# Message pass of a graph kernel: the repeat-redirected cells of a tile are written ahead of the scan, with one semaphore for each slot of their ring

## What is computed

```python
# layer 1 (message pass), batch norm over all edges inside _mlp
node_feat = _mlp(x, W_node, b_node, g_node, beta_node)
edge_feat = _mlp(edge_attr, W_edge, b_edge, g_edge, beta_edge)
message = concatenate([x[row], x[col], edge_feat], axis=1)
message = _mlp(message, W_msg, b_msg, g_msg, beta_msg)
agg = segment_sum(message, col)
# layers 2 and 3: two SAGE convolutions each, over the same edges
agg = segment_sum(x[src], dst) / max(degree, 1);  out = agg @ Wl.T + b + x @ Wr.T
```

## Time and profile before

| | us |
|---|---|
| median of 3 runs | 5384.24 (5378.25 to 5390.44) |
| the profiled execution | 5342.66 |
| its span | 5340.8 |
| its message pass, 1474 to 3361 | 1887 |
| PE / DVE / ACT / POOL busy over the span | 3187.4 / 2666.4 / 1564.4 / 2506.9 |

### The profile page before, as it was taken

One profiled execution on the slowest core, in us unless ns is written; L12 is line 12 of the kernel. 1 busy time (PEld: TensorE's weight loads), 2 busy tenths in 40 slices (PEclk: granted clock), 3 DMA queues, 4 the chain that ended last, 5 costly groups with the idle time before them and its releaser, 6 DMA issues.

```text
span 5340.8 us, 69053 instructions
## 1 busy us (share of the span) xinstructions
PE 3187.4 (60%) x18737; PEld 2331.0 (44%) x18737; DVE 2666.4 (50%) x5882; ACT 1564.4 (29%) x3677; POOL 2506.9 (47%) x2580
## 2 busy tenths in 40 slices
PE   1555555553755555455455555311129999999999
PEld 0333333332633333333333334210017777778777
DVE  4888888886554555445454554700001154433333
ACT  1777777773222222222222222200000011111000
POOL 7666666664455565556556565777750000000000
PEclk9999999999966666666766676555559999999999
DMA  5565555653233344333344334200017756676776
GB/s 186 192 199 195 197 197 192 202 195 104 57 101 104 100 107 103 102 101 100 104 105 103 101 99 109 81 2 0 12 37 266 256 197 248 234 262 250 257 274 230
DMA packets 387448, 796.21 MB, mean 149 GB/s; under 512 B 207412, under 2 KB 264600, under 8 KB 361128
## 3 DMA queue, kind: packets, MB, share of 16 engines
q1 hardware_dynamic: 239330, 586.35, 32.8%
q0 software_dynamic: 82320, 90.28, 8.3%
q10 hardware_dynamic: 65718, 118.62, 5.8%
HBM read 581.03 MB, written 213.92 MB: 149 GB/s over the span
## 4 chain that ended last, share of the span: by engine, by line
PE 29%; issue 17%; another core or an unknown queue 14%; DVE 5%; ACT 3%; SPq 3%; DMA 1%; ACTq 1%; DVEq 0%; POOL 0%
PE ps L1166 17%; PE ps L1096 6%; SPq L633 2%; ACT ps L1215 2%; PE ps L920 1%; PE ps L927 1%; PE ps L926 1%; DVE area L1664 1%; DVE second L1629 1%; ACT out_ring L1239 1%; DMA attr<-attr_parts 1%; ACTq L1241 1%; ACT dump L1219 1%; PE ps L1049 1%
## 5 line engine op out<-in xcount | busy, mean ns | idle before, releaser
L779 POOL DMA_INDIRECT area<-relu_table,early x784 | 741.5, 946 | 400.6 <-issue 214.9
L938 PE MATMUL ps<-ident,area 96*128 96x96 f32 x2352 | 436.4, 353 | 801.5 <-issue 296.0
L779 POOL DMA_INDIRECT area<-src_table,early x784 | 752.7, 960 | 240.6 <-issue 237.9
L938 PEld LDWEIGHTS ps<-ident,area 96*128 96x128 f32 x2352 | 347.6, 210 | 926.6 <-issue 651.0
L1664 DVE TENSOR_TENSOR_SCAN area<-flags,area,ps 96x512 f32<-96x512 int8 x196 | 249.7, 1274 | 906.1 <-ACT dump L1219 732.8
L1166 PE MATMUL ps<-second,area 128*128 128x288 bf16 x5194 | 650.7, 286 | 0.2 <-DVE second L1811 0.2
L788 POOL DMA_INDIRECT adj<-copies_ring,cell_ring x392 | 390.0, 995 | 531.7 <-DVE cell_ring L1645 425.3
L1166 PEld LDWEIGHTS ps<-second,area 128*128 128x128 f16 x5194 | 508.3, 98 | 127.6 <-DVE second L1811 0.5
L1629 DVE SCALAR_TENSOR_TENSOR second<-second,area,ps 128x512 bf16<-128x512 f32 x784 | 538.6, 744 | 0.0
L920 PE MATMUL ps<-second,w_ef_scaled 96*96 96x512 f32 x392 | 307.0, 876 | 297.3 <-ACT second L1263 158.7
L1096 PE MATMUL ps<-early,area 128*128 128x288 bf16 x2401 | 327.5, 293 | 261.9 <-issue 261.9
(11 more groups left out here) (330 smaller groups left out, 4687.0 us busy)
## 6 DMA issues: line engine op xcount, KB each, us to landing
area<-adj SPq DMA_DIRECT2D x147, 1632.0 KB
area<-adj SPq DMA_DIRECT2D x55, 1568.0 KB
adj<-early SPq DMA_DIRECT2D x102, 816.0 KB
soft_sums<-out_ring ACTq DMA_DIRECT2D x196, 384.0 KB
second<-key_dram SPq DMA_DIRECT2D x98, 512.0 KB
area<-dst_table SPq DMA_DIRECT2D x784, 48.0 KB
sums<-out_ring ACTq DMA_DIRECT2D x196, 192.0 KB
second<-caps_dram SPq DMA_DIRECT2D x98, 192.0 KB
```

The source lines that it names most:

```text
L779: pool.indirect_dma_start(out=src_rows[:, s, c % CH, :], out_offset=None, in_=gather_table[p], in_offset=bass.IndirectOffsetOnAxis(ap=src_ ...
L938: last = nc.tensor.transpose(ps[:, b, c * F:(c + 1) * F], r[:, (s * CH + c) * P:(s * CH + c + 1) * P], ident[0:F, 0:F])
```

## The change

DVE's order in the message pass becomes `place`, `count_copies` and `redirect` of tile t+1, then `scan` of tile t. `adj_made` becomes four semaphores, one for each slot, and a fifth counts the two joint scatters (L806). To have semaphores for these, others are merged (`hot_made` with `counts_kept`, `lasts_counted` with `lasts_summed`, `ef_coefs_made` with `msg_bias_made`), and an unused one goes. The instructions are otherwise the same.

```diff
-        zeros_made, adj_cleared, marked, redirected, adj_made = (
-            sem("zeros_made"), sem("adj_cleared"), sem("marked"), sem("redirected"), sem("adj_made"))
+        zeros_made, adj_cleared, marked, redirected, joint_ones_made = (
+            sem("zeros_made"), sem("adj_cleared"), sem("marked"), sem("redirected"), sem("joint_ones_made"))
+        adj_made = [sem(f"adj_made{s}") for s in range(RING)]
...
-                            in_=copies_ring[:, s, c:c + 1], in_offset=None).then_inc(adj_made, 16)
+                            in_=copies_ring[:, s, c:c + 1], in_offset=None).then_inc(adj_made[s], 16)
...
-                            in_=one_h[:, :], in_offset=None).then_inc(adj_made, 16)
+                            in_=one_h[:, :], in_offset=None).then_inc(joint_ones_made, 16)
...
-                    pool.wait_ge(adj_made, 16 * (EARLY + EXT))
+                    for s in range(RING):
+                        pool.wait_ge(adj_made[s], 16 * NOW * EI)
+                    pool.wait_ge(joint_ones_made, 16 * EXT)
                     pool.sem_inc(adj_ready, 1)
...
                     dve.wait_ge(e["counted"], t + 1)
-                    wait(dve, adj_made, (t - RING + 1) * (16 * NOW))
+                    wait(dve, adj_made[s], u * (16 * NOW))
...
-                def place_and_count(u, s):
+                def place_and_redirect(u, s):
                     place(u, s)
                     count_copies(u, s)
-
-                def scan_and_redirect(u, s):
-                    scan(u, s)
                     redirect(u, s)
...
-                    over_tiles(dve, place_and_count, scan_and_redirect)
+                    over_tiles(dve, place_and_redirect, scan)
```

More of the change, by code:

```diff
@@ L355, in build @@
         starts_made = sem("starts_made")
-        lasts_landed, hot_made, lasts_counted, counts_kept, lasts_summed, chunk_found = (
-            sem("lasts_landed"), sem("hot_made"), sem("lasts_counted"), sem("counts_kept"), sem("lasts_summed"),
+        lasts_landed, lasts_ready, lasts_summed, chunk_found = (
+            sem("lasts_landed"), sem("lasts_ready"), sem("lasts_summed"),
             sem("chunk_found"))
@@ L362, in build @@
         index_made, relu_made = sem("index_made"), sem("relu_made")
-        ef_coefs_made, ef_bias_summed, msg_bias_made = sem("ef_coefs_made"), sem("ef_bias_summed"), sem("msg_bias_made")
+        coefs_made, ef_bias_summed = sem("coefs_made"), sem("ef_bias_summed")
         diags_made, rows_spread = sem("diags_made"), sem("rows_spread")
@@ L403, in build @@
         out_landed = [sem(f"out_landed{b}") for b in range(2)]
-        conv = sems("conv", "summed_up reduced extended joined posted turned evicted projected zkept split kept centred rooted"
+        conv = sems("conv", "summed_up reduced extended posted turned evicted projected zkept split kept centred rooted"
                             " floored expd")
@@ L862, in _ @@
             pe.wait_ge(consts_made, 2)
-            pe.wait_ge(hot_made, 1)
+            pe.wait_ge(lasts_ready, 1)
             for c in range(HC):
                 last = nc.tensor.matmul(bank(0, P, NT), hot_lo[:, :, c], hot_hi[:, :, c], start=c == 0, stop=c == HC - 1)
-            last.then_inc(lasts_counted, 1)
-            pe.wait_ge(counts_kept, 1)
+            last.then_inc(lasts_summed, 1)
+            pe.wait_ge(lasts_ready, 2)
             nc.tensor.matmul(bank(1, P, NT), tri[:, :], counts, start=True, stop=True)
@@ L954, in _ @@
                 elif kind == MESSAGE:
-                    pe.wait_ge(ef_coefs_made, 1)
+                    pe.wait_ge(coefs_made, 1)
                     nc.tensor.matmul(bank(2, F, 1), W["W_ef"][:, :], t_ef[:, :], start=True, stop=True)\
@@ L1280, in _ @@
                     coef_root(2)
-                    act.wait_ge(msg_bias_made, 1)
+                    act.wait_ge(coefs_made, 2)
                     over_tiles(act, relu_features, relu_message)
@@ L1437, in _ @@
             v.tensor_tensor(hot_lo, last_lo.unsqueeze(1).to_broadcast([P, P, HC]), iota_lo[:, :, :], ALU.is_equal)\
-             .then_inc(hot_made, 1)
-            dve.wait_ge(lasts_counted, 1)
-            v.tensor_copy(counts, bank(0, P, NT)).then_inc(counts_kept, 1)
+             .then_inc(lasts_ready, 1)
             dve.wait_ge(lasts_summed, 1)
+            v.tensor_copy(counts, bank(0, P, NT)).then_inc(lasts_ready, 1)
+            dve.wait_ge(lasts_summed, 2)
             chain.do(v.tensor_copy(total[:, :], bank(6, P, NT)))
@@ L1698, in _ @@
                     norm_coefs(1, ef_sum[:, :], ef_sq[:, :], n_edges, col["g_edge"], col["beta_edge"], s_ef, t_ef)
-                    v.tensor_scalar(w_ef_scaled[:, :], W["W_ef"][:, :], s_ef[:, :], None, ALU.mult).then_inc(ef_coefs_made, 1)
+                    v.tensor_scalar(w_ef_scaled[:, :], W["W_ef"][:, :], s_ef[:, :], None, ALU.mult).then_inc(coefs_made, 1)
                     dve.wait_ge(node[0]["nh_squared"], NG)
@@ L1702, in _ @@
                     dve.wait_ge(ef_bias_summed, 1)
-                    v.tensor_tensor(msg_bias[:, :], bank(2, F, 1), col["b_msg"][:, :], ALU.add).then_inc(msg_bias_made, 1)
+                    v.tensor_tensor(msg_bias[:, :], bank(2, F, 1), col["b_msg"][:, :], ALU.add).then_inc(coefs_made, 1)
                 start_from_zero()
```

## The result

The changed kernel takes 5192.62 us (median of 4 runs, 5190.61 to 5195.28) against 5387.34 us for the kernel before (4 runs beside it, 5378.25 to 5393.46): a ratio of 0.9639, 95% interval 0.9626 to 0.9651, 194.7 us less. Forecast were 5218 us and a range of 5085 to 5400. The profiled execution of the changed kernel took 5191.9 us, its span is 5190.1.

A forecast was written before the change was run, and what follows sets the result against it. POOL's queue was taken to bound the message pass, with 425.3 us of waiting. The profiled 5342.66 us less 166, other terms 0, gave 5176.7; the median's 41.6 us offset made it 5218 us, range 5085 to 5400.

The forecast's parts named there:

- What bounds the kernel: Message pass: POOL's queue is the stage, 1466.6 us of DMAs and issue plus 425.3 us waiting for DVE's cells.
- Step (1): POOL in the message pass: the wait for cells goes, shorter stops for `turned` remain, 81 to 98 at 2.9 us.
- rival 2: POOL's wait only changes its name, to `turned`: 147 stops at 2.9 us, 5384 us in all; chance 0.11.
- the term of 166: Message pass: the forecast gain in us, the middle between 141 (98 stops) and 190 (81 stops).
- From the profiled execution to the median: Whole kernel: the runs' median is 41.6 us above the profiled execution, a difference carried over to the forecast.
- Step (2): DVE's four small redirect operations move ahead of a scan that waits for ACT: counted 0, 0 to +74 us for the range.
- Step (3): DVE's wait for a free slot moves with the redirect; the scatters asked for were issued long before: 0 us.
- Steps (4) and (5): Merged semaphores and four extra waits cost under 1 us; nothing behind the message pass catches the gain.
- The signs: Expected profile: cell wait near zero, 235 to 285 us before gathers, pass some 1720 us; wrong if window loads usually exceed 15.
- rival 1: Fewer POOL stops in the message pass: half left gives 5075 us, none left 4959 us; chance 0.20.
- Rival 3: Slower: POOL stops once for each tile in the message pass, 196 x 2.9 = 568 us of waiting, 5527 us; chance 0.17.

The follow-up runs named there:

- no_pool_dmas: Changed kernel with POOL's DMAs left out of the message pass except the first four gathers, and the waits on them: 4495.86 us.
- pool_memsets_b: As no_pool_dmas, but POOL does two memsets in place of each DMA left out: 4781.02 us, beside 5347.08 for the kernel before.
- after_third: The changed kernel itself, run a third time: 4503.74 us beside 4507.4 for the kernel before, ratio 0.9994.
- after_again: The changed kernel itself, run a second time: 5166.56 us beside 5347.08 for the kernel before, ratio 0.9658.
- slots_only: Changed kernel with DVE's old order (scan of t, then redirect of t), keeping the new semaphores: 5385.35 us, ratio 1.0007 to the kernel before.
- behind_scan: Changed kernel with the redirect of tile t+1 right behind the scan of tile t, not ahead of it: 5191.56 us, ratio 0.9649 to the kernel before.

## Why the prediction was right, step by step

**What bounds the kernel.** POOL's queue is the message pass: work and waits fill the 1733 us of the changed kernel as they filled the 1887 before. Right. That POOL's stream holds the others up is borne out: with the DMAs gone (`no_pool_dmas`) or replaced (`pool_memsets_b`) there is no late word. In the kernel before, a score whose row ends while POOL stands is taken up 1.6 us later on the average (42 tiles), one whose row ends while POOL streams 9.4 us later (154 tiles). That word comes through only in a stop would be too much: in the changed kernel 58 of the 180 scores taken up over 1 us late are taken up while POOL streams. By the Trainium skill's page Perfetto Trace Analysis, section on the per-instruction lifecycle, the end of a TensorE row is computed; the prediction weighed whether the lateness was PE's own time, and the runs decide against it, `after_third` most plainly: the same matmuls, the same computed ends, and ACT 0.12 us behind them. How the stream holds word up is not shown.

**Step (1), the stop.** Right in its mechanism at each point: the wait for the cells 7 us, the new wait in front of the gather, `turned` next in line, 3.6 us less from word to POOL. Two sizes were off, and nearly cancel, which is luck. The stops were taken as 81 to 98 at 2.9 us; they are 125 at 2.2 us, one for 1.57 tiles (196/125) and not for 2 to 2.42. The sum, 277.9 us, lies in the 235 to 284 named. The price was mis-sized by taking the long end for all: in POOL's timeline I count 59 stops after six DMAs, mean 1.6 us, and 66 after twelve, mean 2.7 us. The prediction's own step had the lower price in it: stops of 425.3/81 = 5.25 us, less 3.6 us, are 1.65. Why a stop after one tile's DMAs is shorter is not shown. The number moved as rival 2 feared. By rival 2's price of 2.9 us a stop for 1.57 tiles would have left 363 us and a gain of only 63.

What the step gained has to be read from executions that are alike. From the first to the last scan row the pass takes 1885.9 us in the profiled execution before and 1721.4 in the one after, 164.5 less (the table by stage has 154, since its window begins 12 us ahead of the changed kernel's first scan). That this meets the 166 forecast is chance. The execution before (5342.66 us) is as long as the runs of the kernel before beside `after_again` (5344 to 5356), and shorter than all of its runs beside the result (5378 to 5393). Against 1885.9 stands the pass of `after_again`, 1705.3: 180.6 less, with the medians 180.5 apart. Against 1721.4 stands the pass of `slots_only` (5381.15 us), 1908.6: 187.2 less, where the medians of the result are 194.7 apart and those of `behind_scan` 187.7. So the term of 166 measures 181 to 187.

A part of this was left out of the sum. Each wait has the 0.30 us of issue in it that POOL would spend anyway. In POOL's timeline before I count 90 stops with 439.6 us in all, 412.6 without that issue; in that of `after_again` 114 with 266.3, 232.1 without it. The difference is 180.5 us, the gain of the pass.

**From the profiled execution to the median.** The prediction made its sum on an execution 41.6 us under the median and carried that difference over unchanged. It is not a constant: the kernel before is 40.3 us longer beside the result than beside `after_again` (5387.34 and 5347.08), the changed kernel only 26.1 (5192.62 and 5166.56). So of the 28.7 us by which 166 falls short of 194.7, about half is this carrying over, and about half the stop's term.

**Step (2), the redirect on DVE.** 0, as counted: it stands ahead of a scan that waits for ACT 447.9 us in the pass. The page SBUF — State Buffer of the Trainium skill, section "two separate sides", is narrower than the prediction has it: a DVE operation with two SBUF inputs gets GpSimd's port only against a GpSimd operation that reads SBUF. No run here shows the rule at work: POOL's gathers and scatters take 960 and 995 ns on average before and after, and those that run beside a redirect are not longer (gathers 955 ns, scatters 992 in the changed kernel).

**Step (3), the wait for a slot.** 0 in the trace of the changed kernel. In condition B it exists, 276.6 us in 153 times, and costs nothing there, as the ratio of 0.9994 bears out; DVE has time to spare.

**Steps (4) and (5).** Right: `slots_only` puts the semaphores at 1.0007, and the stages behind are 539 and 1443 us, against 539 and 1446 in `slots_only`.

**The signs.** Window loads took over 15 us in one of the 98 pairs (17.7), so not as a rule; two of them:

```profile
2498.06 13.57 SPq L634 DMA_DIRECT2D area<-dst_table  x8
...
2554.88 8.24 SPq L634 DMA_DIRECT2D area<-dst_table  x8
```

SP is more steadily slow now, 9.0 us on the average, where the kernel before had 10.3 and was over 15 us in 24 of its 98 pairs. PE waits 175.8 us for its attribute loads. The prediction argued against rival 1 from the 19.77 us of the earlier trace rows, 9.9 us a tile; that was one of the longest, and the mean of before is 5.1 us a tile.

**The rivals.** Rival 1's case, a POOL that never stops, is what condition B shows: a pass of 1482 us, where the prediction worked out 1467, without the issue time inside the waits. It says nothing for the change, since the kernel before had it there as well. Rival 3 had a premise that came half true, more and shorter stops with one tile after half of them, but these cost 1.6 us each and not 2.9.

**Open.** What makes conditions A and B (groups of runs on the same chip fell in either); by what path POOL's stream delays semaphores and SP in A and not in B; whether in A, in the pass, the waits on its DMAs have a part in it; why the number of stops settled at 125; what fewer DMAs or a forced stop for each tile would give in A.

## What to carry to other kernels

Add up work, issue and waits of each queue: the queue whose sum is the stage is the one to shorten, whatever its busy share. When a wait is taken away, look for the one that it had absorbed and price that by how long the word is in coming, and expect the number of stops to change too. Compare profiled executions that are alike, here by the time of the kernel before beside each: two that were not gave 164.5 us where like ones gave 181 to 187.

## What had not been expected of the hardware

The same kernels take 5347 to 5387 or 4505 to 4507 us, by where or when they ran. The message pass without POOL's DMAs is alike in both (1066.6 us), and with them a score is taken up 5.1 us after PE's row in A and 0.12 us in B, so what differs there is what POOL's stream of indirect DMAs does to the others. The stage behind the pass shows it most plainly. There POOL scatters the late columns for over 500 us and SP loads `adj` for the first convolution. The changed kernel's SP queue, in condition A and in B (`after_third`, its view to 3000 us):

```profile
3301.16 445.83 SPq L676 DMA_DIRECT2D area<-adj  x5
```

```profile
2906.98 91.77 SPq L676 DMA_DIRECT2D area<-adj  x13
```

Five loads in 446 us or thirteen in 92, but SP's loads are not slow by themselves. The first four start within 4 us in both; the fifth waits for PE's first product. What is late is word, and by more than in the pass. From who waited for whom in that stage, in A:

```profile
DVE early L1824 <- remote: 148.3, 7, 31.0
DVE whole L1836 <- remote: 134.4, 1, 134.4
```

PE projects the nodes in thirteen rounds from PE to DVE to ACT and back. In A seven of them take 33.6 us each, with DVE taking up a result some 19 us after PE's row ended; in B a round takes about 3 us. These rounds wait for no DMA, only for PE, DVE and ACT, so here the late word needs no wait on a DMA. The first product of the convolution ends by its row at 3656.4, and DVE takes it up at 3744.3, 88 us later, with SP's fifth load 1.3 us behind. In B the convolution runs beside the scatters. By stage, in B:

```profile
2814.00:3352.00 538.00, 335.86 (x2320) 253.60 (x2321) 140.30 (x267) 27.57 (x49) 406.50 (x404) 0.79 0.41 137
3352.00:4494.00 1142.00, 1097.30 (x8912) 876.76 (x8909) 435.37 (x1618) 119.71 (x420) 36.77 (x38) 0.99 0.67 239
```

PE is busy 336 of the 538 us against 82 in A, and the rest takes 1142 us, not 1443. Both are cut at the same length behind the pass, and what PE has done in it in B is 301 us off the end. In all the same kernel is 239 us longer in the message pass (1721 against 1482), 301 us in the stages behind it, and 155 us in the softmax pass (1487 against 1332), where POOL also gathers with indirect DMAs. That the late word is all of it was tested for the message pass alone.
